# Self-attention of a decoder layer: probabilities as the moving operand in four column tiles, the subtraction of maxima on POOL, one exponential per four heads

## The reference

```python
q = (hidden_states @ Wq).reshape(b, s, 32, 16)
kv = hidden_states @ Wkv
k, v = (kv[..., :16], kv[..., 16:])                      # one key and value head for all 32
scores = einsum('bqhd,bkd->bhqk', q, k) * 16 ** -0.5
bias = slopes[:, None, None] * (pos[None, None, :] - pos[None, :, None])
scores = where(pos[None, :] <= pos[:, None], scores + bias[None], -inf)
attn = softmax(scores, axis=-1)
out = einsum('bhqk,bkd->bqhd', attn, v).reshape(b, s, 512)
return out @ Wo
```

## Time and profile before

| | |
|---|---|
| median of three runs | 1029.2 us |
| profiled execution, span from first to last instruction | 1029.7 us |
| PE busy | 1003.1 us (97%) |
| DVE, ACT, POOL busy | 581.3, 428.1, 381.6 us (56%, 42%, 37%) |
| mean granted TensorE clock | 0.992 of 2.4 GHz |

### The profile page before, as it was taken

How to read it: one execution, slowest core, us unless ns; L and a number is a source line. 1 busy time by engine, 2 the same in 40 slices (tenths; PEclk the granted TensorE clock), 3 DMA queues, 4 the chain that set the end, 5 groups by cost and what they waited for, 6 DMA issues and landing times. The chain is left out here.

```text
span 1029.7 us, 16071 instructions
## 1 busy us (share of the span) xinstructions
PE 1003.1 (97%) x5260; PEld 822.9 (80%) x5260; DVE 581.3 (56%) x973; ACT 428.1 (42%) x1239; POOL 381.6 (37%) x375
## 2 busy tenths in 40 slices
PE   5999999989999999999999999999999999999998
PEld 3787777876888888888888888888887778888787
DVE  3765555636776666767666666766765852222101
ACT  2777666751533433533533434434334433332100
POOL 7422222253642642643634534626424222222100
PEclk8999999989999999999999999999999999999999
DMA  6000000211110210210210201201100022221001
GB/s 199 12 11 11 11 10 10 62 52 52 50 54 1 73 32 0 71 31 0 74 27 20 72 10 31 61 10 49 43 1 32 1 62 61 61 69 47 11 31 41
DMA packets 45699, 39.98 MB, mean 39 GB/s; under 512 B 3617, under 2 KB 34465, under 8 KB 45665
## 3 DMA queue, kind: packets, MB, share of 16 engines
q1 hardware_dynamic: 45280, 38.48, 12.7%
q0 software_dynamic: 384, 1.05, 0.3%
HBM read 37.43 MB, written 2.10 MB: 38 GB/s over the span
## 5 line engine op out<-in xcount | busy, mean ns | idle before, releaser
L624 PE MATMUL bank<-cross_wo_hl,cross_outT_hl 128*128 128x512 f32 x768 | 191.7, 398 | 1.0 <-POOL cross_wo_hl L618 0.6
L624 PE MATMUL bank<-hsT_hl,cross_wqkv_hl 128*128 128x512 f32 x768 | 188.2, 394 | 0.0
L624 PEld LDWEIGHTS bank<-cross_wo_hl,cross_outT_hl 128*128 128x128 f32 x768 | 143.1, 188 | 35.5 <-POOL cross_wo_hl L618 1.6
L624 PEld LDWEIGHTS bank<-hsT_hl,cross_wqkv_hl 128*128 128x128 f32 x768 | 141.9, 188 | 29.3
L938 ACT ACTIVATE cross_scores<-cross_scores,cross_negmax 128x128 f32<-128x128 f32 x256 | 99.8, 391 | 127.1 <-DVE cross_negmax L876 127.1
L798 POOL TENSOR_TENSOR cross_qT<-rotated,rotated_other_half 128x512 f32<-128x512 f32 x64 | 82.8, 1293 | 162.0 <-DVE rotated_other_half L840 162.0
L624 PE MATMUL bank<-hsT_hl,ff_gate_upT_hl 128*128 128x512 f32 (+1 forms) x528 | 126.3, 395 | 0.5 <-DVE ff_gate_upT_hl L1140 0.5
L624 PEld LDWEIGHTS bank<-hsT_hl,ff_gate_upT_hl 128*128 128x128 f32 (+1 forms) x528 | 96.3, 186 | 21.9 <-DVE ff_gate_upT_hl L1140 0.8
L948 ACT CAST cross_outT_hl<-bank 128x512 fp32r<-128x512 f32 x64 | 37.1, 579 | 143.4 <-PE bank L624 142.5
L838 DVE TENSOR_TENSOR rotated<-bank,cosT 128x512 f32<-128x512 f32 x80 | 55.2, 690 | 71.4 <-PE bank L624 71.2
L624 PE MATMUL bank<-ctxT_hl,cross_wqkv_hl 128*128 128x512 f32 x384 | 94.3, 394 | 1.1 <-PEq L74 1.1
(11 more groups left out here) (121 smaller groups left out, 1565.7 us busy)
## 6 DMA issues: line engine op xcount, KB each, us to landing
staged_rows<-in_wq SPq DMA_DIRECT2D x32, 256.0 KB, 2.8
staged_rows<-in_wo SPq DMA_DIRECT2D x32, 256.0 KB, 2.7
staged_rows<-in_wg SPq DMA_DIRECT2D x10, 256.0 KB, 2.6
staged_rows<-in_wu SPq DMA_DIRECT2D x10, 256.0 KB, 2.8
staged_rows<-in_wd SPq DMA_DIRECT2D x10, 256.0 KB, 3.0
ctx_tok<-in_ctx SPq DMA_DIRECT2D x8, 256.0 KB, 2.6
staged_rows<-in_wk SPq DMA_DIRECT2D x8, 256.0 KB, 3.1
staged_rows<-in_wv SPq DMA_DIRECT2D x8, 256.0 KB, 3.1
```

Source lines behind the costliest of these rows:

```text
L624: i = nc.tensor.matmul(out, stationary[:, a], moving[:, b], start=(first and k == 0), stop=(last and k == 2))
```

## The change

The change is inside `self_attention`, with the constants that it reads.

- **Bias.** The host passes the bias of heads 0 to 3, 128 x 512; it is loaded by DMA, POOL's 32 instructions go. DVE adds it with `scalar_tensor_tensor`: `bias * 0.5 ** s + scores`.
- **Maxima and exponential.** POOL adds the negated maximum to `S` in place (`shift`), one 128 x 512 instruction per step. ACT then computes one exponential of 128 x 512 per step, in place, and does so one step later in its list than before. `S` and `negmax` have four buffers in place of two, `PR` is gone.
- **Values.** `PT` has four buffers. Every four steps (`pv`), four products stand behind each other on PE: 32 stationary columns (16 of values, 16 of ones), 512 moving columns (four heads' transposed probabilities), the output of the j-th at partitions 32j to 32j + 31 of one bank `OT`. ACT copies `OT` to `oT`, PE transposes it back in four 128 x 128 transposes into `OQ` (`o_transposes`), and `normalise` reads that. The values of one sequence alone stand in `v`; those of the next wait in `v_next` until ACT copies them.
- **Order.** POOL's `hs_of`, `keys_by_head`, `rstd_of_x` and `xn_of` stand at given steps among the shifts. The indirect DMAs stand ahead of the shifts of the last sequence, the weight pieces between those shifts.

```diff
-    SC, TB, OB, G = ps[0:2], ps[2:4], ps[4:6], ps[6:8]
+    SC, TB, OT, OQ, G = ps[0:2], ps[2:4], ps[4], ps[5], ps[6:8]
...
-        bias = sb("alibi_bias", [P, HEADS, P])
-        rel = sb("relative_position", [P, P])
+        bias = sb("alibi_bias", [P, QUAD * P])
...
-        v = sb("self_v_and_ones", [P, SEQS, HD1 + 1])
-        S = sb("self_scores", [P, 2, QUAD, P])
-        PR = sb("self_probs", [P, 2, QUAD, P])
-        negmax = sb("self_negmax", [P, 2, QUAD])
-        PT = sb("self_probsT", [P, 2, QUAD, P])
-        rsum = sb("self_rsum", [P, HEADS])
+        v = sb("self_v_and_ones", [P, 2 * HD1])
+        v_next = sb("self_v_of_next", [P, HD1])
+        S = sb("self_scores", [P, 4, QUAD, P])
+        negmax = sb("self_negmax", [P, 4, QUAD])
+        PT = sb("self_probsT", [P, 4, QUAD * P])
+        oT = sb("self_outT_by_step", [P, QUAD * P])
+        rsum = sb("self_rsum", [P, HEADS // 2])
...
+            sp.dma_start(bias[:], io["constants"][:, 0:QUAD * P]).then_inc(sem["bias_loaded"], 16)
...
-            pool.wait_ge(sem["rel_loaded"], 16)
-            for h in range(HEADS):
-                nc.gpsimd.tensor_scalar(bias[:, h, :], rel[:], slopes[h], None, ALU.mult).then_inc(sem["bias"], 1)
-                if h == 15:
-                    pool.wait_ge(sem["head_of_row_loaded"], 16)
-                    keys_by_head(0)
-                    rstd_of_x(1, 2)
-                    xn_of(1)
+            pool.wait_ge(sem["head_of_row_loaded"], 16)
+            keys_by_head(0)
...
+            def shift(b, s):
...
+                n = STEPS * b + s
+                pool.wait_ge(sem["max1"], n + 1)
+                nc.gpsimd.tensor_tensor(S[:, s % 4], S[:, s % 4], negmax[:, s % 4, :].unsqueeze(2).to_broadcast([P, QUAD, P]), ALU.add).then_inc(sem["shifted1"], 1)
...
-            body(0)
-            rstd_of_x(2, SEQS)
-            body(1)
-            body(2)
-            with pool.Fori(3, SEQS - 1) as b:
+                for s in range(STEPS):
+                    shift(b, s)
+                    if s == 1 and since(b, 2):
+                        hs_of(b - 2)
+                    if s == 5 and not since(b, SEQS - 1):
+                        keys_by_head(b + 1)
+                    if s == 5 and not since(b, 1):
+                        rstd_of_x(2, SEQS)
+                    if s == 6 and not since(b, SEQS - 2):
+                        xn_of(b + 2)
+            for b in range(3):
                 body(b)
-            body(SEQS - 1)
+            with pool.Fori(3, SEQS - 2) as b:
+                body(b)
+            body(SEQS - 2)
...
-            for j in range(PIECES):
-                piece_low(nc, pool, m, sem, j % SLOTS, j, m["wqkv_hl"][:, j])
-            body(SEQS)
+            for s in range(STEPS):
+                shift(SEQS - 1, s)
+                if s == 1:
+                    hs_of(SEQS - 3)
+                if s >= 2:
+                    piece_low(nc, pool, m, sem, (s - 2) % SLOTS, s - 2, m["wqkv_hl"][:, s - 2])
...
-                o = OB[i][:, 0:16 * (HD1 + 1)].rearrange("p (h d) -> p h d", h=16)
+                o = OQ[:].rearrange("p (h s d) -> p h s d", h=QUAD, s=HALF)
...
-                dve.wait_ge(sem["pv1"], STEPS * b + HALF * (i + 1))
+                dve.wait_ge(sem["o_transposed"], 2 * b + i + 1)
...
-                    if s == 3 and since(b, 1):
-                        normalise(b - 1, 1)
...
-                        if since(b, 1) or s >= 2:
-                            dve.wait_ge(sem["exp1"], n - 1)
-                        if not since(b, 1):
-                            dve.wait_ge(sem["bias"], QUAD * (s + 1))
-                        nc.vector.tensor_tensor(S[:, s % 2], SC[s % 2][:].rearrange("p (h k) -> p h k", h=QUAD),
-                                                bias[:, QUAD * s:QUAD * s + QUAD, :], ALU.add).then_inc(sem["biased1"], 1)
+                        if since(b, 1) or s >= 4:
+                            dve.wait_ge(sem["probs_transposed1"], n - 3)
+                        if not since(b, 1) and s == 0:
+                            dve.wait_ge(sem["bias_loaded"], 16)
+                        nc.vector.scalar_tensor_tensor(out=S[:, s % 4], in0=bias[:].rearrange("p (h k) -> p h k", h=QUAD), scalar=0.5 ** s,
+                                                       in1=SC[s % 2][:].rearrange("p (h k) -> p h k", h=QUAD), op0=ALU.mult, op1=ALU.add).then_inc(sem["biased1"], 1)
                         dve.wait_ge(sem["biased1"], n + 1)
-                        nc.vector.tensor_reduce(negmax[:, s % 2, :], S[:, s % 2], AX.X, ALU.max, negate=True).then_inc(sem["max1"], 1)
+                        nc.vector.tensor_reduce(negmax[:, s % 4, :], S[:, s % 4], AX.X, ALU.max, negate=True).then_inc(sem["max1"], 1)
...
+                    if s == 3 and since(b, 1):
+                        normalise(b - 1, 1)
...
-                nc.scalar.copy(v[:, bass.ds(c, 1), 0:HD1], G[0][:, P:P + HD1].unsqueeze(1))
+                    act.wait_ge(sem["v_in_use"], c)
+                nc.scalar.copy(v_next[:], G[0][:, P:P + HD1]).then_inc(sem["v_next"], 1)
...
+                    if (since(b, 1) or s >= 1) and (scores or s < 1):
+                        act.wait_ge(sem["shifted1"], n)
+                        nc.scalar.activation(S[:, (s - 1) % 4], S[:, (s - 1) % 4], ACT.Exp).then_inc(sem["exp1"], 1)
...
-                        if since(b, 1) or s >= 4:
-                            act.wait_ge(sem["pv1"], n - 3)
-                        nc.scalar.copy(PT[:, s % 2], TB[s % 2][:].rearrange("p (h k) -> p h k", h=QUAD)).then_inc(sem["probsT1"], 1)
+                        if since(b, 1) or s >= 6:
+                            act.wait_ge(sem["pv1"], 2 * b + s // 4 - (s % 4 < 2))
+                        nc.scalar.copy(PT[:, (s - 2) % 4], TB[s % 2][:]).then_inc(sem["probsT1"], 1)
+                    if (s == 3 and back) or (s == 7 and scores):
+                        h = 2 * b + (s == 7)
+                        act.wait_ge(sem["pv1"], h)
+                        if since(b, 1) and not (isinstance(h, int) and h == 1):
+                            act.wait_ge(sem["o_transposed"], h - 1)
+                        nc.scalar.copy(oT[:], OT[:]).then_inc(sem["o_copied"], 1)
+                    if s == 3 and scores:
+                        act.wait_ge(sem["v_next"], b + 1)
+                        if back:
+                            act.wait_ge(sem["pv1"], 2 * b)
+                        nc.scalar.copy(v[:, 0:HD1], v_next[:]).then_inc(sem["v_in_use"], 1)
...
-                    if scores:
-                        act.wait_ge(sem["max1"], n + 1)
-                        if since(b, 1) or s >= 2:
-                            act.wait_ge(sem["probs_transposed1"], n - 1)
-                        for j in range(QUAD):
-                            e = nc.scalar.activation(PR[:, s % 2, j, :], S[:, s % 2, j, :], ACT.Exp, bias=negmax[:, s % 2, j:j + 1])
-                        e.then_inc(sem["exp1"], 1)
...
+            def pv(h, seqs):
+                pe.wait_ge(sem["probsT1"], HALF * h + HALF)
+                if isinstance(h, int) and h == 0:
+                    pe.wait_ge(sem["ones_ready"], 1)
+                else:
+                    pe.wait_ge(sem["o_copied"], h)
+                pe.wait_ge(sem["v_in_use"], seqs)
+                for j in range(HALF):
+                    i = nc.tensor.matmul(OT[32 * j:32 * (j + 1), :], v[:], PT[:, j, :], start=True, stop=True)
+                i.then_inc(sem["pv1"], 1)
+            def o_transposes(h):
+                pe.wait_ge(sem["o_copied"], h + 1)
+                if not (isinstance(h, int) and h == 0):
+                    pe.wait_ge(sem["attn"], h)
+                for i in range(QUAD):
+                    e = nc.tensor.transpose(OQ[:, i * P:(i + 1) * P], oT[:, i * P:(i + 1) * P], ident[:])
+                e.then_inc(sem["o_transposed"], 1)
...
-                            i = nc.tensor.transpose(TB[s % 2][:, j * P:(j + 1) * P], PR[:, s % 2, j, :], ident[:])
+                            i = nc.tensor.transpose(TB[s % 2][:, j * P:(j + 1) * P], S[:, (s - 2) % 4, j, :], ident[:])
...
-                    if (since(b, 1) or s >= 3) and (scores or s < 3):
-                        r = (s - 3) % STEPS
-                        owner = b if s >= 3 else b - 1
-                        pe.wait_ge(sem["probsT1"], n - 2)
-                        if r % HALF == 0 and (since(b, 2) or owner >= 1):
-                            pe.wait_ge(sem["attn"], 2 * owner - 1 + r // HALF)
-                        for j in range(QUAD):
-                            c = (QUAD * (r % HALF) + j) * (HD1 + 1)
-                            i = nc.tensor.matmul(OB[r // HALF][:, c:c + HD1 + 1], PT[:, r % 2, j, :], v[:, bass.ds(owner, 1), :].rearrange("p b d -> p (b d)"),
-                                                 start=True, stop=True)
-                        i.then_inc(sem["pv1"], 1)
+                    if s == 2 and back:
+                        pv(2 * b - 1, b)
```

(10 more changed lines are left out.)

27 lines of the change are left out of this document (10 added, 17 removed).

## The result

The changed kernel takes 1023.8 us (median of four runs, 1022.4 to 1024.9), the kernel before 1030.5 in the runs beside it; the ratio is 0.9931, with a 95% interval of 0.9914 to 0.9948. The forecast was 1037, slower: the sign was wrong, and the time lies near where the first rival (1025) put it. The windows of the kernel after, with the columns of the earlier trace rows: five steady sequences, last sequence and end of the block, and all that follows.

A forecast was written before the change was run, and what follows sets the result against it. PE was taken to bound five steady sequences, a chain of waits the end. First sequence +1.9 and +1.0, second -0.5, steady -0.7, end +6.1 gave +7.8 us: forecast 1037, its own range 1031 to 1044, overall 1022 to 1055.

The forecast's parts named there:

- first rival: All four column tiles stream at once, P = 0.85: faster, -3.9 us in all, 1025 us; chance 0.27.
- P: Time of one group of four column-tile value products on PE: taken as 2.13 us, bounds 0.85 and 3.41.
- the forecast's own sum for a steady sequence: Third to seventh sequence: 19.48 + 0.86 + 4.26 + 0.9 + 0.35 = 25.85 us against 26.0, -0.15 each.
- its order of starts: PE records start in program order, a tile's second after its first; eight records take five slots of 0.427 us.
- Before, nothing waited for it: Last sequence: claimed nothing waited for POOL's eight indirect DMAs (10.0 us) in their old place.
- The end +6.1: Last sequence and end of block: +3.3 POOL's pace, +1.8 to the division, +1 lower clock; +6.1 us together.
- neither had the last word in these sequences: Steady sequences: easing ACT (8 x 0.7 us of exponentials less) and DVE (nothing less) was claimed to gain nothing.
- First sequence, +2.9: Second sequence's scores +1.9 us later behind POOL's work ahead of step 6's shift, plus 1.0 for lower clock.
- Steady waits: New PE waits per steady sequence: 0.9 us at step 0's transposes, 0.35 in the sum for the key product.
- The 0.9 us of step 2: Each sequence: PE's transposes in step 2 wait near 0.9 us on ACT's exponential, behind POOL's shift.
- the sizes of the three new instructions: DVE's new bias form 0.68 us, POOL's shift 1.04, ACT's one exponential per step 0.60.
- the third rival, the clock: Clock falls within the steady sequences: +21 us on the forecast, 1058 us; chance 0.08.

The follow-up runs named there:

- two_tiles: Changed kernel with the four value products, from the second group on, sent to column tiles 0, 1, 0, 1 (half the output stale); ratio 1.0036 to the kernel before.
- pv_twice: Changed kernel with each group of four column-tile products issued twice, output unchanged; 1033.9 us, ratio 1.0031 to the kernel before.
- one_tile: Changed kernel with all four value products, from the second group on, in column tile 0 (three quarters of output stale); 1060.6 us, ratio 1.0292 to before.
- before_tables: Kernel before, with POOL's eight indirect DMAs issued a sequence earlier in its list; 1025.0 us, ratio 0.9951.
- neither: Changed kernel with old value products and no POOL shift, keeping small bias table, four buffers, later exponential, new POOL order; 1021.1 us, 9.7 us faster than before.
- before_copy: Kernel before, with ACT copying the next sequence's transposed q ahead of the exponentials of step 7 in every sequence; 1027.7 us, ratio 0.9970.
- exp_by_head: Changed kernel without POOL's shift: ACT computes the exponential head by head with the negated maximum as bias; 1007.1 us, ratio 0.9776 to before.

## Why the prediction was wrong

- **The step that failed is P**, the time of four column-tile products. 2.13 us was taken, 1.00 measured. The bounds held; the choice between them did not. It rested on an order of the records of a float32 product which no row showed, and on being the middle. At two `pv` per sequence this is 2.3 us per sequence. With P = 1.00 the forecast's own sum for a steady sequence, 25.85, becomes 23.6, and 24.7 with the longer waits of its first rival; 23.95 was measured.
- **P alone turns the sign.** The changed kernel with a P of 1.84 (`two_tiles`) or 1.86 us (`pv_twice`) is slower than the kernel before, 1.0036 and 1.0031; with 1.00 it is faster. A straight line between these puts the turn near P = 1.6 (an estimate); the forecast had it near 1.3. From 1.86 to 3.55 us (`one_tile`) one us of P costs 16 us, so 2.13 would have given some 1038 us (an estimate). That this is so near the forecast is luck: in `pv_twice` the end of the block takes 44.74 us (194.80 to 239.54), 12.2 more than the 32.53 of `before_tables`, where the forecast booked 6.1; the 6.8 us that it did not hold, below, hide this.
- **The first rival's 1025 is partly luck as well.** It had P right in kind, but the steady sequences at -1.5 each (measured -2.0), the end at +4.0 (+2.4) and the first sequence at +2.9 (+1.0 and +1.6), and held no part of the 9.7 us either.
- **A rule that was read both ways.** The Trainium skill (TensorE: Matmul & The Clock Gate, Part 3: Packing small matmuls) says that products in different column tiles run at once, and the trace agrees: four tiles are 3.55 / 1.00 = 3.5 times as fast as one. The prediction took 0.85 from it, and 2.13 from its order of starts laid on the two records of one product; `two_tiles` (1.84, not 2.28) rules the second reading out.
- **"Before, nothing waited for it" was false.** The 3.24 us wait of ACT for a DMA, until 219.46, stood in the trace before, just ahead of the stretch at the end that was read, and the clock that was low at 222 us came with it: in the profile of `before_tables` it is 1.00 there. The forecast counted where the DMAs would go and not what they left behind: 6.8 us in that profile, 6.9 in that of `neither`. "The end +6.1" is therefore two terms: the shift behind the DMAs costs 9.1 (41.73 against 32.61), the old place of the DMAs gives back 6.8 to 6.9, in all +2.4.
- **The move of one copy on ACT was not counted**, although the 0.18 us "issue" gap ahead of the scores at 119.32 stood in PE's timeline: 0.39 us per steady sequence (`before_copy`, 129.67 to 127.73 for five). Of ACT and DVE the forecast said that "neither had the last word in these sequences"; for ACT that was wrong at this one place.
- **First sequence, +2.9:** the mechanism was right (POOL's keys and statistics ahead of the shift of step 6, and a wait of nearly 4 us: 3.52), the size less: +1.0 and +1.6 in two profiles. The clock blurs it. `before_tables` has the same instructions there as the kernel before, but a clock of 1.00 instead of 0.62 in 19 to 25 us, and takes 20.43 us instead of 22.61.
- **Steady waits:** 1.30 us per sequence measured, 1.25 forecast. The 0.9 us of step 2 does not fall where it was expected: in the sequence shown there is a wait of 0.56 for DVE's `x` ahead of the `xn` transposes (0.82 in the next sequence), and a delay of 0.16 ahead of the step's own. That wait is no part of POOL's chain and stands in `exp_by_head` as well.
- **Right:** the wait at the start of the last sequence (8, measured 8.76), the sizes of the three new instructions, the unchanged 793 us behind the block, the clock below 1.00 in the first, second and last sequence and 1.00 in the five between (the third rival, the clock, is out).
- A small one in the base: in the later runs of the kernel before, a run takes 1.8 us more than its span (1031.49 and 1029.7, for one). The profile before (1029.7) therefore belongs to a run of some 1031.5, near the longest of the three shown (an estimate), and not to one 0.5 us off the median.

## What to carry to other kernels

Where a term is bounded by a factor of four and the sign hangs on it, its midpoint is no estimate: write both sums and weigh what is known of the mechanism. When a change moves an instruction, ask what stood behind it in its old place before asking what it delays in the new one; an old wait of 3 us was worth 6.8 here, with the clock that fell behind it. Part by part, this change was three: the tiles (-13 to -20 us), a new order on POOL and ACT (-10), and the shift (+16 to +22); only the sum looked like 0.7%, and leaving out the shift gives 2.2 to 2.3%.

## What the runs showed of the hardware

- Float32 products into 32 columns with 512 moving columns: 0.427 us times the records of the fullest tile plus 0.15 us per visit (1.00, 1.84, 1.86 and 3.55 us for 2, 4, 4 and 8). The transposes ahead of a visit take 0.53 to 0.58 us to its first record instead of 0.43, and this is not in the 0.15. The Trainium skill (TensorEngine Tiling (Array Packing), Key Properties) says that a change of the tiling mode drains the engine; the 0.15 us would fit that, but no run tells it from another cause. At the lower clock level (0.50) a `pv` took 1.86 us (197.95 to 199.81), less than twice 1.00, as if the 0.15 did not grow; this is one reading.
- Eight indirect DMAs in a row held POOL for 10.0 us in each of three places (205.55 to 215.56 before, 185.15 to 195.13 after, 188.87 to 198.86 in `before_tables`), and with it what is queued behind them on POOL.
- Behind a wait of 1.84 us on PE the granted clock stood at 0.50 from 222 to 232 us in the kernel before, though PE was busy for 9.1 of these 10 us.
- Four exponentials of 128 x 128 with a bias of their own keep ACT busy for 1.28 us (`exp_by_head`), one of 128 x 512 for 0.64. The saving of 0.64 us costs 1.04 us of POOL and one more handover, and only the steady sequences with old products (25.55 with the shift, 25.56 without) show no loss from it.
